# A perceiver layer in one program: output weights loaded behind four turned halves, two remainders ahead of the rotations, all of V projected ahead of its products

## The reference

```python
q = (query @ wq)...            # 32 heads of 128; rotated by position
k = (key @ wk)...              # 8 groups of 128; rotated
v = (value @ wv)...            # 8 groups of 128
scores = einsum('bhqd,bhkd->bhqk', q, k) / sqrt(128)
attn = softmax(scores + mask)                 # over 2048 context rows
out = einsum('bhqk,bhkd->bhqd', attn, v)
return out @ wo
```

## Time and profile before

| what | value |
| --- | --- |
| median of three runs | 748.7 us |
| the profiled execution, its own time | 749.1 us |
| its span in the trace | 747.4 us |
| PE busy | 667.1 us (89%) |
| DVE busy | 570.6 us (76%) |
| ACT busy | 447.7 us (60%) |
| POOL busy | 328.3 us (44%) |
| DMA queue q1, share of 16 engines | 56.6% |

### The profile page before, as it was taken

How to read it: one execution, slowest core, us unless ns; L and a number is a source line. 1 busy time by engine, 2 the same in 40 slices (tenths; PEclk the granted TensorE clock), 3 DMA queues, 4 the chain that set the end, 5 groups by cost and what they waited for, 6 DMA issues and landing times.

```text
span 747.4 us, 11651 instructions
## 1 busy us (share of the span) xinstructions
PE 667.1 (89%) x3615; PEld 564.1 (75%) x3615; DVE 570.6 (76%) x1179; ACT 447.7 (60%) x633; POOL 328.3 (44%) x159
## 2 busy tenths in 40 slices
PE   8998599499869949976994997799999999999998
PEld 7886488388658838855883885689998899998987
DVE  5998379449837945983794597487897999999996
ACT  4484457268445726845572583656486767676672
POOL 2354313603431350342235035130059888788884
PEclk9999699789969979996996999899999999999999
DMA  8619416712932670393277138367465978788630
GB/s 317 249 43 218 107 70 149 165 51 84 218 105 70 164 184 19 97 222 86 70 175 176 32 98 193 84 232 305 150 225 218 403 303 341 290 324 328 262 140 16
DMA packets 137781, 130.47 MB, mean 175 GB/s; under 512 B 119200, under 2 KB 120352, under 8 KB 128032
## 3 DMA queue, kind: packets, MB, share of 16 engines
q1 hardware_dynamic: 137760, 130.21, 56.6%
HBM read 100.51 MB, written 0.33 MB: 135 GB/s over the span
## 4 chain that ended last, share of the span: by engine, by line
PE 60%; DMA 13%; SPq 12%; DVE 6%; issue 5%; POOL 2%; ACT 1%; DVEq 0%; POOLq 0%
PE bank L455 15%; PE bank L456 14%; PE bank L457 14%; PE bank L697 9%; SPq L344 9%; DMA halves<-halves 8%; DMA halves<-high 4%; PE bank L809 3%; DVE halves L1230 2%; SPq L338 1%; DMA wqo_raw<-in_wq 1%; PE bank L552 1%; DVE probs L1263 1%; SPq L369 1%; POOL w_gate_lo L1722 1%
## 5 line engine op out<-in xcount | busy, mean ns | idle before, releaser
L1687 POOL TENSOR_TENSOR wqo_lo<-wqo_raw,wqo_hi 128x2048 fp32r<-128x2048 f32 x14 | 64.0, 4574 | 169.1 <-ACT wqo_hi L865 169.1
L455 PE MATMUL bank<-pt_hi,v_hi 128*128 128x512 f32 (+1 forms) x144 | 62.3, 433 | 69.7 <-ACT pt_hi L913 60.0
L1345 DVE CAST pt_lo<-halves 128x512 fp32r<-128x512 f16 x112 | 47.4, 429 | 100.4 <-DMA halves<-high 57.6
L1674 POOL TENSOR_TENSOR k_lo<-rope_a,k_hi 128x512 fp32r<-128x512 f32 x32 | 61.8, 1931 | 128.2 <-ACT k_hi L883 128.2
L913 ACT ACTIVATE pt_hi<-halves 128x512 fp32r<-128x512 f16 x112 | 69.3, 631 | 71.5 <-DMA halves<-high 49.6
L455 PEld LDWEIGHTS bank<-pt_hi,v_hi 128*128 128x128 f32 x144 | 31.4, 218 | 78.2 <-issue 72.5
L1263 DVE CUSTOM_DVE_ANT_0 probs<-bank,mask_sb 128x512 f32<-128x512 f32 x128 | 80.9, 684 | 0.0
L1717 POOL TENSOR_TENSOR w_out_lo<-w_out_sb,w_out_hi 128x2048 fp32r<-128x2048 f32 x16 | 73.4, 4590 | 5.0 <-ACT w_out_hi L1083 4.9
L1722 POOL TENSOR_TENSOR w_gate_lo<-w_gate_sb,w_gate_hi 128x2048 fp32r<-128x2048 f32 x14 | 64.7, 4621 | 15.2 <-ACT w_gate_hi L1075 15.2
L1230 DVE SCALAR_TENSOR_TENSOR halves<-probs,high 128x2048 f16<-128x2048 f32 x28 | 65.8, 2370 | 0.0
L883 ACT ACTIVATE k_hi<-rope_a 128x512 fp32r<-128x512 f32 x32 | 20.1, 628 | 68.1 <-DVE rope_a L1205 68.1
(11 more groups left out here) (227 smaller groups left out, 1798.0 us busy)
## 6 DMA issues: line engine op xcount, KB each, us to landing
w_hs_sb<-in_w_hs SPq DMA_DIRECT2D x16, 1024.0 KB, 4.9
w_out_sb<-in_w_out SPq DMA_DIRECT2D x16, 1024.0 KB, 6.3
w_gate_sb<-in_w_gate SPq DMA_DIRECT2D x16, 1024.0 KB, 4.9
wqo_raw<-in_wq SPq DMA_DIRECT2D x8, 1024.0 KB, 4.7
mask_sb<-in_mask SPq DMA_DIRECT2D x8, 1024.0 KB, 4.8
wqo_raw<-in_wo SPq DMA_DIRECT2D x8, 1024.0 KB, 6.2
decay<-decay_rows SPq DMA_DIRECT2D x16, 512.0 KB, 6.8
ctx_raw<-in_ctx_t SPq DMA_DIRECT2D x3, 1024.0 KB, 11.1
```

Of the source, the lines that this page charges most:

```text
L455: pe.matmul(dst, left_hi, right_hi, start=first, stop=False)
L1674: pool.tensor_tensor(k_lo[:, blk], rope_a[:, (b + 1) % 2, :], k_hi[:, blk].bitcast(F32), ALU.subtract)\
L1687: pool.tensor_tensor(wqo_lo[:, :, :], wqo_raw[:, :, :], wqo_hi[:, :, :].bitcast(F32), ALU.subtract)\
```

## The change

- SP: `turn_first_heads` now issues the low halves of heads 0 and 1, then their high halves, and then the load of `wo`; a new `turn_last_heads` issues the low halves of heads 2 and 3 and then their high halves. The load of `wk` comes behind all eight transposes.
- DVE: `low_half(3)` stands right behind `low_half(2)`, ahead of `k_rotate(1)`.
- PE: the fourth V block is projected ahead of the products with V; the turn of V block 0 stands after the seventh product step; behind the products stands only the turn of block 1, then the output projection.
- ACT and DVE: the high and low part of V block 0 are made in the middle of the products (`v_high` after step 8, `v_low` after step 10). `attn_low` is two instructions of two heads each, and PE waits for each pair of heads.
- POOL: the low part of `wo` is made in four quarters, two after the low parts of K blocks 0 and 1, and two after those of blocks 2 and 3.

The diff:

```diff
+VALUE_TURN = 6
...
             def turn_first_heads(g):
                 turn_low(g, 0)
                 turn_low(g, 1)
+                turn_high(g, 0)
+                turn_high(g, 1)
                 sp.wait_ge(s["qproj_ready"], g + 2)
                 sp.dma_start(wqo_raw[:, :, :], wo[g]).then_inc(s["wo_in"], 16)
-                turn_high(g, 0)
-                turn_high(g, 1)
+
+            def turn_last_heads(g):
                 turn_low(g, 2)
+                turn_low(g, 3)
                 turn_high(g, 2)
-
-            def turn_last_head(g):
-                turn_low(g, 3)
                 turn_high(g, 3)
-                reload_mask(g)
 
             with sp.Fori(2, G) as g:
                 turn_first_heads(g - 2)
+                turn_last_heads(g - 2)
                 sp.wait_ge(s["kproj_ready"], KB * g)
                 sp.dma_start(wk_raw[:, :, :], wk[g]).then_inc(s["wk_in"], 16)
-                turn_last_head(g - 2)
+                reload_mask(g - 2)
                 sp.wait_ge(s["vproj_ready"], KB * g)
...
             def attend(g):
                 project_v_block(g + 1, 1)
                 project_v_block(g + 1, 2)
+                project_v_block(g + 1, 3)
                 pe.wait_ge(s["v_lo_ready"], KB * (g + 1))
                 for t in range(KT):
...
                         .then_inc(s["pv_step"], 1)
+                    if t == VALUE_TURN:
+                        transpose_v_block(g + 1, 0)
...
             def project_out(g):
                 pe.wait_ge(s["wo_lo_ready"], g + 1)
-                pe.wait_ge(s["attn_lo_ready"], g + 1)
                 pe.wait_ge(s["inverse_ready"], g + 1)
                 for h in range(HG):
+                    pe.wait_ge(s["attn_lo_ready"], 2 * g + h // 2 + 1)
...
                 attend(g)
-                transpose_v_block(g + 1, 0)
-                project_v_block(g + 1, 3)
                 transpose_v_block(g + 1, 1)
                 project_out(g)
...
+                    if t == VALUE_TURN + 2:
+                        v_high(g + 1, 0)
                     if t == SUM_STEPS[1]:
...
                     if b == 0:
                         attn_high(g - 1)
-                    v_high(g, b)
+                    else:
+                        v_high(g, b)
...
                 low_half(g - 1, 2)
+                low_half(g - 1, 3)
                 k_rotate(g, 1)
-                low_half(g - 1, 3)
                 k_rotate(g, 2)
...
+                    if t == VALUE_TURN + 4:
+                        v_low(g + 1, 0)
...
             def attn_low(g):
-                dve.wait_ge(s["attn_hi_ready"], g + 1)
-                dve.tensor_tensor(attn_lo[:, :, :].rearrange("p h t -> p (h t)"), pv_bank[:, :],
...
+                for pair, cols in enumerate(HALVES):
+                    two = slice(2 * pair, 2 * pair + 2)
+                    dve.wait_ge(s["attn_hi_ready"], g + 1)
+                    dve.tensor_tensor(attn_lo[:, two, :].rearrange("p h t -> p (h t)"), pv_bank[:, cols],
...
                 attn_low(g)
-                v_low(g + 1, 0)
+                v_low(g + 1, 1)
                 add_head(g, 0)
-                v_low(g + 1, 1)
...
+            def wo_low_quarters(g, quarters):
+                for h in quarters:
+                    if h == 0:
+                        pool.wait_ge(s["wo_hi_ready"], g + 1)
+                    last = pool.tensor_tensor(wqo_lo[:, h, :], wqo_raw[:, h, :], wqo_hi[:, h, :].bitcast(F32),
+                                              ALU.subtract)
+                    if h == HG - 1:
+                        last.then_inc(s["wo_lo_ready"], 1)
...
-                k_low(g)
-                wqo_low(s["wo_hi_ready"], s["wo_lo_ready"], g - 1)
+                k_low(g, range(2))
+                wo_low_quarters(g - 1, range(2))
+                k_low(g, range(2, KB))
+                wo_low_quarters(g - 1, range(2, HG))
```

More of the change, by code:

```diff
@@ L375, in _ @@
             turn_first_heads(G - 2)
-            turn_last_head(G - 2)
+            turn_last_heads(G - 2)
+            reload_mask(G - 2)
             sp.wait_ge(s["oproj_ready"], HG * (G - 1))
@@ L617, in last_project_out @@
                 dst, cols = (oq_bank, bank[0])[half], HALVES[half]
-                pe.wait_ge(s["attn_lo_ready"], G + pair)
+                pe.wait_ge(s["attn_lo_ready"], 2 * (G - 1) + pair + 1)
                 for h in (2 * pair, 2 * pair + 1):
@@ L1367, in attn_low @@
             def attn_low(g):
-                dve.wait_ge(s["attn_hi_ready"], g + 1)
-                dve.tensor_tensor(attn_lo[:, :, :].rearrange("p h t -> p (h t)"), pv_bank[:, :],
-                                  attn_hi[:, :, :].rearrange("p h t -> p (h t)").bitcast(F32), ALU.subtract)\
-                    .then_inc(s["attn_lo_ready"], 1)
+                for pair, cols in enumerate(HALVES):
+                    two = slice(2 * pair, 2 * pair + 2)
+                    dve.wait_ge(s["attn_hi_ready"], g + 1)
+                    dve.tensor_tensor(attn_lo[:, two, :].rearrange("p h t -> p (h t)"), pv_bank[:, cols],
+                                      attn_hi[:, two, :].rearrange("p h t -> p (h t)").bitcast(F32), ALU.subtract)\
+                        .then_inc(s["attn_lo_ready"], 1)
             dve.wait_ge(s["xres_ready"], 16)
@@ L1668, in split_weight, with k_low @@
                     .then_inc(lo_done, 1)
-            def k_low(g):
-                for b in range(KB):
+            def k_low(g, blocks=range(KB)):
+                for b in blocks:
                     blk = slice(b * 512, (b + 1) * 512)
```

## The result

| what | before | after |
| --- | --- | --- |
| median of four runs each, us | 748.32 (747.66 to 750.16) | 710.35 (707.75 to 711.36) |
| ratio after / before, 95% interval | | 0.9484 (0.9453 to 0.9514) |
| the profiled execution, us | 749.1 | 707.75 |
| its span, us | 747.4 | 706.0 |
| mean granted clock of PE | 0.936 | 0.99 |

The change is faster by 5.2%. The forecast was 689 us in a range of 669 to 705: the sign was right, the size was not, and the time lies 5 us above the range. 38 us came of 59.5. The ratios of the experiments are to runs of the kernel before that were taken beside them (medians 747.3 and 746.5 us). Two executions in a slower state, one of the transposes alone (907.75 us) and one of the kernel before beside it (3645.45 us), are left out of medians and ratios.

A forecast was written before the change was run, and what follows sets the result against it. PE was taken to wait for the turned high parts before the products with V, 69.7 us in all. Gains of 5.24, 0.8 and 2.4 made 8.5 us a round, 59.5 in seven rounds: 689 us, range 669 to 705.

The forecast's parts named there:

- Costed at nothing: Side effects given no cost: later `wo`, ACT's wait, POOL's quarters (0 to 1 us on the products' start, counted 0).
- M to T: Stretch from a round's first mask addition to its first low half issued; taken as practically unchanged, 13.55 us.
- The transposes: SP's queue: `wo` behind four transposes holds head 2, yet the last high half lands at 206.6, 5.2 us earlier.
- no hold: Rival: head 2's low half does not wait behind `wo`; 11.4 us a round gained, 669 us; chance 0.07.
- transposes in series: Rival: the second four transposes take 4.2 to 4.3 us each, landing later than before; some 743 us; chance 0.09.
- T to L: Stretch from first low half issued to last high half landed; forecast 23.1 us, 28.3 before.
- The pace of 2.1 us: SP's queue: transposes behind each other land every 2.1 us, taken from three landings in the kernel before.
- The clock: PE's clock falls in the 1.5 us gap before the products, costing 1.5 us a round (ends 0 and 2.8).
- the V block in the gap before the products: PE runs the fourth V block from some 203.1 to 205.8, in the idle stretch; 1.5 us idle instead of 10.
- the tail: From the products' end to the next round's first mask addition: 6.1 us in place of 8.6, a gain of 2.4.
- another wait of more than 2 us a round: Sign the forecast is wrong: such a new wait on PE, for low parts of K, `wo_lo` or `wq`.
- the five stretches: Parts of a round: M to T 13.55, T to L 23.1, landing to products 0.76, products 12.9, their end to next mask 6.1.

The follow-up runs named there:

- the transposes alone: Kernel before with only SP's new transpose order and `low_half(3)` ahead of `k_rotate(1)`; V, POOL and the end of the round as before: 738.95 us, ratio 0.9892.
- the best version: Kernel after with two late `wo` low-part quarters on DVE, POOL's `wk` split held until the last cast, and `wv` split before `wq`: 693.77 us, ratio 0.9292.
- the quarters undone: Kernel after with the low part of `wo` whole again on POOL, behind all four low parts of K: 723.92 us, ratio 0.9693.

## Why the prediction was wrong

**The step that failed: "Costed at nothing".** The prediction asked of POOL's new order only whether the low parts of K would come late for PE, and took "0 to 1" us for the start. It did not ask what else on POOL the products slide under when they start 5 us sooner. The casts on DVE now lie over the late quarters and the split of `wk`, and where they meet, the two engines shut each other out: casts 7.6 to 10.4 us a round in sum in place of 6.9, the products up to 1.45 us after the landing in place of 0.75, and 13.0 and 13.6 us long in two of the three rounds whose clock stayed up (11.44 is what they take then with POOL out of the way). The same holds of the term that was carried over as unchanged, M to T: the split of `wv` lies over the first low half, 0.5 us a round more than in the kernel before and 0.67 more than without it. Taking POOL out of both brings the ratio from 0.9484 to 0.9292, 14 us (16.6 by the medians). In the traces it is 2.2 us a round, 15 us: 0.67 in M to T, 0.33 before the products and 1.26 in them, where some 0.5 is the clock by an estimate: it fell in four rounds of the kernel after and in two of the best version, and a fall cost 1.6 us (13.0 less 11.4). This cause is shown.

A page of the Trainium skill states the mechanism: "SBUF — State Buffer", section "Who interferes with whom", says that VectorE and GpSimd share a pair of ports as an exclusive lock, held for a whole instruction by whoever issues first, that casts can be among the operations that take it, and that an operation with two inputs in SBUF contends with GpSimd's reads. The traces agree: 4.37 us for two casts that began in a POOL instruction of 4.50. By that rule quarters are better than one whole instruction, since one that waits then waits for no more than a quarter; the runs have that too (723.92 to 710.35), though that edit also moved two of the quarters ahead of the casts, and no run parts the two.

**The transposes: right mechanism, size off.** Head 2 is held behind `wo`; the rivals of no hold (which the prediction calls the first, but lists second) and of transposes in series are out. The term T to L was too small at both of its parts. The hold's end came 15.5 us after T in the mean, where 14.6 was forecast, and the four transposes behind it took 9.2 in place of 8.5. In the third round it was 15.0 and 8.9; there the last one took 4.84 to land where 4.27 was taken. The sum is 24.7 in the mean for 23.1 (24.0 to 25.1, and 26.0 in the first round), some 11 us in seven rounds. The pace of 2.1 us was the mean of three landings of the kernel before, two high halves and a low one, 1.95, 2.48 and 1.81 us apart. In the third round after, two low and two high halves landed 1.88, 2.01, 2.58 and 2.33 us apart: 2.2 in the mean, the two high halves slower than the two low ones. The stretches of both kernels (granted clock, DMA share, GB/s at the end of a row), before:

```profile
193.76:200.07 6.31, 6.03 (x27) 4.71 (x26) 6.20 (x8) 2.44 (x2) 2.62 (x1) 1.00 1.08 224
```

and after:

```profile
180.40:194.70 14.30, 12.19 (x51) 9.04 (x50) 12.17 (x14) 4.19 (x5) 6.88 (x6) 1.00 1.08 237
```

The DMA engines are as busy in the one as in the other (share 1.08), so busier DMA engines don't explain the slower pace; why the high halves took longer, and why `wo` landed later behind its four transposes, was not tried, and stays open.

**The clock: over-costed, and hid the rest.** The forecast put 1.5 us of lost clock on each round, from one row. The stretches of the products, second and third round after (PEclk, the granted clock, is the third value from the end):

```profile
136.90:150.80 13.90, 13.41 (x52) 9.91 (x52) 8.94 (x17) 9.47 (x17) 3.04 (x3) 0.88 0.23 92
195.40:209.10 13.70, 12.30 (x52) 8.85 (x52) 9.81 (x17) 10.06 (x18) 4.43 (x4) 1.00 0.25 96
```

The mean is 1.00 in three rounds, behind gaps of 3.29, 1.23 and 2.20 us, and 0.87 or 0.88 in four, behind gaps of 2.17 to 2.39. In the best version it is 1.00 in five rounds, all behind gaps of 1.6 to 1.8, and 0.87 in two:

```profile
193.30:204.70 11.40, 11.40 (x52) 9.11 (x52) 6.48 (x17) 9.94 (x18) 0.87 (x2) 1.00 0.31 115
...
417.60:430.60 13.00, 13.00 (x52) 10.23 (x52) 6.46 (x16) 9.89 (x18) 0.00 (x0) 0.87 0.23 81
```

So the 1.5 was about the right price of a fall (1.6 here, 13.0 less 11.4) and wrong as a certainty: the gap of 1.6 us in the earlier trace rows lost the clock, five of nearly that length did not. In the kernel after, products of 13.16 look like the 12.9 of the forecast, but by another cause: the slow casts stand where the lost clock was to have stood, wholly in the third and the fifth round.

**Right:** the V block in the gap before the products, and the tail (6.04, 6.1 forecast). The gap itself is as forecast in the third round alone (1.23 for 1.5); in the others it is 2.2 to 3.3. The forecast's condition, "another wait of more than 2 us a round" on PE, was met in the transposes alone and with the quarters undone (2.0 to 3.2 and 1.4 to 2.9 us more before the products); in the kernel after the wait is there in smaller pieces.

In the best version the five stretches differ from the forecast by -0.3, +1.7, 0, -1.0 and -0.1 us, in all 2 us in seven rounds (693.8 us for 689): the transposes cost 12 us more than forecast, the products give 7 of them back, and M to T another 2. So that version comes near the forecast in part by luck, by errors that cancel; and the miss of 17.5 us in the rounds of the kernel after is some 15 for POOL and 12 for the transposes, less those 9.

## What to carry to other kernels

When a change moves the start of a stage by some us, list what every other engine does in the new place, not only whether it is ready in time: work on POOL that was over before the stage may now lie under DVE's. Two engines that can shut each other out belong on one timeline, and the one that is off the critical path should be cut in small instructions or ordered around the other's critical stretch. A total that agrees term by term in size may still be right by two errors; check the cause of each term (here the clock) in the rows.

## What the hardware showed that was not expected

- DVE and POOL exclude each other by whole instructions in these forms: two casts that take 0.76 us alone took 4.37 under a POOL instruction of 4.50, and a low half 3.03 in place of 2.29. Not every DVE instruction is held: in the third round after, a rotation's last addition, both inputs in SBUF, took 1.56 us beside POOL's `k_lo` (0.69 alone), while its three products before it, each with an input in a PSUM bank, kept their 0.68 to 0.69 beside POOL's quarters of `wo`.
- In the best version the granted clock stayed at 1.00 behind five gaps of 1.6 to 1.8 us on PE, and the mean of the products fell to 0.87 behind two of 2.1 and 3.5; in the kernel after it stayed up behind one of 3.3, and of two gaps of 2.20 one kept it and one lost it. The length of the gap alone doesn't tell which.
- A transpose of 0.5 MB behind a load of 1 MB takes 5.4 us to issue in place of 1.9; with 0.25 MB the pair of them took 4.8 in place of 7.2.
